# Expert weights of a job in four loads, each asked for when its half of the buffer is used up

## The reference

```python
def experts(x, gate_scores):                 # x: 16 samples x 256 tokens x 256 channels
    topk_w, topk_i = top_k(gate_scores, 2)   # two of four experts for each sample
    topk_w = topk_w / (topk_w.sum() + 1e-8)
    for e in range(4):
        h = gelu(x @ ew1[e] + eb1[e])        # 256 -> 1024
        y = h @ ew2[e] + eb2[e]              # 1024 -> 256
        out += w_be[:, e] * mask[e] * y
    return x + out + gelu(x @ sw1 + sb1) @ sw2 + sb2   # the shared expert, for all samples
```

## Time and profile before

| | us |
|---|---|
| median of three timed runs | 1384.66 (1384.63 to 1385.9) |
| the profiled execution's own time | 1386.06 |
| its span, first to last instruction | 1384.2 |
| expert jobs, first to last matmul start | 608.6 to 1008.1 |
| shared expert and recurrent network | from 1011.0 to the end |
| TensorE busy | 1227.4 (89% of the span) |
| VectorE busy | 883.5 (64%) |
| ScalarE busy | 633.3 (46%) |
| bytes read from HBM in the whole kernel | 160.66 MB |

### The profile page before, as it was taken

The page is one execution under the profiler, slowest core; times in us unless marked ns, Lnnn a source line. Parts: engine busy times, 40 slices in busy tenths (PEclk is TensorE's granted clock), DMA queues, the critical chain, the costliest instruction groups (busy, mean ns, idle before and its releaser), DMA issues.

```text
span 1384.2 us, 34408 instructions
## 1 busy us (share of the span) xinstructions
PE 1227.4 (89%) x14232; PEld 982.0 (71%) x14232; DVE 883.5 (64%) x2091; ACT 633.3 (46%) x1191; POOL 330.5 (24%) x311
## 2 busy tenths in 40 slices
PE   4489999999997878159899999999999999999996
PEld 2347676767664333049899999999988888888884
DVE  4978787878773499856565565656555555555552
ACT  2267777777775799413233333333323333333331
POOL 2554545454442399600000000000000000000000
PEclk9689999999999899659999999999999999999996
DMA  9212121212123000057888888888810000000000
GB/s 340 91 47 93 47 94 47 93 47 94 47 93 123 1 0 1 15 243 296 324 354 338 335 327 345 358 345 339 337 75 10 18 18 10 18 10 18 10 18 18
DMA packets 37898, 188.29 MB, mean 136 GB/s; under 512 B 3056, under 2 KB 13424, under 8 KB 29040
## 3 DMA queue, kind: packets, MB, share of 16 engines
q1 hardware_dynamic: 37744, 186.10, 35.1%
HBM read 160.66 MB, written 25.17 MB: 134 GB/s over the span
## 4 chain that ended last, share of the span: by engine, by line
PE 48%; DMA 4%; issue 3%; DVE 2%; ACT 0%; SPq 0%; POOLq 0%; POOL 0%; ACTq 0%
PE pr L1387 6%; PE py L1291 4%; DMA w<-weight_halves 4%; PE ph L1275 4%; PE ph L1276 4%; PE ph L1277 4%; PE py L1293 4%; PE py L1292 4%; PE pys L1426 4%; PE pys L1430 4%; PE phs L1413 2%; PE phs L1409 2%; PE phs L1411 2%; PE pys L1428 2%; PE pr L1398 2%
## 5 line engine op out<-in xcount | busy, mean ns | idle before, releaser
L1114 ACT ACTIVATE g<-ph,b 128x256 f32<-128x256 f32 x256 | 121.5, 475 | 273.5 <-PE ph L1277 273.5
L549 DVE TENSOR_REDUCE mx<-pR 128x4 f32<-128x1024 f32 x128 | 156.3, 1224 | 66.0 <-PE pR L707 64.5
L1222 DVE CAST ghi<-g 128x256 fp32r<-128x256 f32 x256 | 74.7, 292 | 154.0 <-ACT g L1114 153.8
L1493 DVE STREAM_TRANSPOSE preT<-pr 128x64 f32<-128x64 f32 x256 | 63.8, 249 | 163.4 <-PE pr L1387 163.0
L1291 PE MATMUL py<-ghi,w 128*128 128x256 f32 x512 | 147.6, 288 | 18.3 <-issue 16.9
L1275 PE MATMUL ph<-xhi,w 128*128 128x256 f32 x512 | 146.3, 286 | 17.3 <-DMA w<-weight_halves 17.3
L1468 ACT ACTIVATE hs<-preT 128x32 f32<-128x32 f32 x256 | 58.7, 229 | 199.6 <-DVE preT L1493 198.1
L1276 PE MATMUL ph<-xlo,w 128*128 128x256 f32 x512 | 145.9, 285 | 0.0
L1277 PE MATMUL ph<-xhi,w 128*128 128x256 f32 x512 | 145.8, 285 | 0.0
L1292 PE MATMUL py<-glo,w 128*128 128x256 f32 x512 | 145.3, 284 | 0.0
L1293 PE MATMUL py<-ghi,w 128*128 128x256 f32 x512 | 145.2, 284 | 0.0
(11 more groups left out here) (195 smaller groups left out, 2981.0 us busy)
## 6 DMA issues: line engine op xcount, KB each, us to landing
w<-weight_halves SPq DMA_DIRECT2D x66, 2048.0 KB, 12.0
weight_halves<-wparts SPq DMA_DIRECT2D x40, 512.0 KB, 4.1
modw<-in_ew SPq DMA_DIRECT2D x32, 256.0 KB, 4.6
xn<-in_x_tok SPq DMA_DIRECT2D x4, 1024.0 KB, 11.8
XT<-in_x_dm SPq DMA_DIRECT2D x2, 2048.0 KB, 14.2
out_dm<-staged SPq DMA_DIRECT2D x16, 256.0 KB, 2.0
modw<-in_sw SPq DMA_DIRECT2D x8, 256.0 KB, 4.3
modw<-in_mod_w SPq DMA_DIRECT2D x1, 768.0 KB, 7.1
```

The lines of the kernel that those rows point to most:

```text
L549: nc.vector.reduce_max(mx[:, :, 2 * j:2 * j + 2].rearrange("p t s -> p s t"), pR[k][:].rearrange("p s (t k) -> p s t k", t=TC), AX.X).then ...
L1114: nc.scalar.activation(g[:, t % RING], ph[t % RING][:, 0:T], ACT.Gelu_apprx_tanh, bias=b1[:, n, f:f + 1]).then_inc(gelu_done, 1)
```

## The change

`load_weights` makes four loads of 1 MB for each job where there were two of 2 MB. The inner width of 1024 is taken in two halves, h = 0 and h = 1 (four ticks each), and for each half the part of `w1` is loaded and then the part of `w2`. Each load has a wait of its own ahead of it: that of `w1` waits until the `up` ticks of that half of job n-2 are done, that of `w2` until its `down` ticks are. The waits in the caller are gone, also for job 32. A partition's half of `w1` is now four runs of 2 KB (high and low part by two halves of the channels), its half of `w2` two runs of 4 KB; before each was one run of 16 KB. The semaphores `w_in` get an index for the half, and TensorE waits at ticks 0 and 4 of a job, in `up` and in `down`, for the half that it goes into. `shared_and_rnn` waits for all four loads of job 32.

```diff
-        w_in = [[sem(st, f"w{w}_in{q}") for q in range(2)] for w in (1, 2)]
+        w_in = [[[sem(st, f"w{w}_in{h}{q}") for q in range(2)] for h in range(2)] for w in (1, 2)]
-        def load_weights(sp, n, src):
-
-            for w, dst, form in ((0, w1, "p v c f -> p (v c f)"), (1, w2, "p v c d -> p (v c d)")):
-                sp.dma_start(dst[:, n % 2].bitcast(fp32).rearrange(form), src[:, w].rearrange("o p v n -> p (o v n)"))\
-                    .then_inc(w_in[w][n % 2], 16)
+        def load_weights(sp, n, src, up, down):
+
+            for h in range(2):
+                lo, hi = h * FC // 2, (h + 1) * FC // 2
+                if n >= 2:
+                    sp.wait_ge(up, FC * (n - 2) + hi)
+                sp.dma_start(w1[:, n % 2, :, :, lo * P:hi * P].bitcast(fp32).rearrange("p v c f -> p (v c) f"),
+                             src[:, 0].rearrange("o p v (c f) -> p (o v c) f", c=DC)[:, :, lo * P:hi * P]).then_inc(w_in[0][h][n % 2], 16)
+                if n >= 2:
+                    sp.wait_ge(down, FC * (n - 2) + hi)
+                sp.dma_start(w2[:, n % 2, :, lo:hi].bitcast(fp32).rearrange("p v c d -> p v (c d)"),
+                             src[:, 1, :, :, lo * D:hi * D].rearrange("o p v n -> p (o v) n")).then_inc(w_in[1][h][n % 2], 16)
...
-                    if n >= 2:
-                        sp.wait_ge(down_done, FC * (n - 1))
-                    load_weights(sp, n, halves[bass.ds(e, 1)])
-                sp.wait_ge(down_done, FC * (JOBS - 1))
-                load_weights(sp, JOBS, halves[NE:NE + 1])
+                    load_weights(sp, n, halves[bass.ds(e, 1)], up_done, down_done)
+                load_weights(sp, JOBS, halves[NE:NE + 1], up_done, down_done)
...
-                        pe.wait_ge(w_in[0][n % 2], 16 * (n // 2 + 1))
+                    if f % (FC // 2) == 0:
+                        pe.wait_ge(w_in[0][2 * f // FC][n % 2], 16 * (n // 2 + 1))
...
-                    if f == 0:
-                        pe.wait_ge(w_in[1][n % 2], 16 * (n // 2 + 1))
-                        if n >= 2:
-                            pe.wait_ge(y_added, n - 1)
+                    if f % (FC // 2) == 0:
+                        pe.wait_ge(w_in[1][2 * f // FC][n % 2], 16 * (n // 2 + 1))
+                    if f == 0 and n >= 2:
+                        pe.wait_ge(y_added, n - 1)
...
-                pe.wait_ge(ex["w_in"][w][BUF], 16 * (TOP * B // 2 + 1))
+                for h in range(2):
+                    pe.wait_ge(ex["w_in"][w][h][BUF], 16 * (TOP * B // 2 + 1))
```

## The result

Four runs of the changed kernel beside four of the kernel before: 1354.67 us (1353.67 to 1359.35) against 1385.28 (1384.63 to 1387.12), 30.6 us less; the ratio is 0.9771, with an interval of 0.9746 to 0.9797. 1356 was forecast, in 1353.5 to 1372. The profiled execution took 1354.25 us, with a span of 1352.5.

A forecast was written before the change was run, and what follows sets the result against it. Late load requests, not DMA rate, were taken to hold back the DMA engines and so TensorE. Terms -25.2 - 2.2 - 1.2 = -28.6 us took the 1384.66 median to 1356.1; own range 1353.5 to 1359, overall 1353.5 to 1372.

The forecast's parts named there:

- (a): Expert weight loads: earlier requests give each half some 18 us from request to use, taking latency out of the sum.
- (b): Expert weight loads in shorter runs: the DMA engines need 10.5 to 10.9 us a job, under TensorE's 11.52.
- R: Time the DMA engines take to move one job's 4.19 MB of weights, taken as 10.5 to 10.9 us.
- the bound of 11.48: Value of R, 11.48 us or 365 GB/s, above which the DMA engines rather than TensorE set the pace.
- (c): Steady expert stage: with weights there, ticks run at 1.44 us throughout; term -25.2 us.
- (d): First expert job: the smaller first load lets the first `up` start earlier; term -2.2 us, from -1.1 to -2.8.
- The bad case: First job: the clock rises at the same absolute time as before, losing half of the 2.2 us again.
- (e): Hand-over to the shared expert: the load wait goes and the barrier is late next; term -1.2 us, not -2.6.
- (f): Added costs: two more TensorE waits a job and 132 SP loads for 66, 1.7 us of issuing in 11.5; term 0.
- The third one: Rival, slower: queue runs dry between loads, each dry spell costing 0.87 us; 14.0 us a job, 1439.5 us; chance 0.08.
- The second: Rival, no change: engines hold one load at a time and pay slow starts; 12.3 us a job, 1383.4 us; chance 0.05.
- The first rival: Rival: R over 11.52, DMA engines set the expert stage's pace; 1359 to 1381 us, 1372 at the bound; chance 0.13.

## Why the prediction was right

**(a) The cause.** That a late request, and not the rate, holds the engines back was right: with 340 GB/s turned into 365 the waits are gone. I had put it on the earlier request alone. The runs show that the halves alone do it too in the steady stage, since they move the need for the second half by four ticks; I had not reckoned that.

**(b) R.** 10.5 to 10.9 us were taken for a job. The rate with a full queue is 394 to 396 GB/s (640 to 680, and both runs with extra loads), 10.6 us. The prediction put the slowest engine 4% over the mean, by instruction fetches that all fall to one. An engine that falls behind is there, but by less: the landings with extra loads come at 12.1 and 13.5 us a job where the mean rate gives 11.9 and 13.3, 1 to 2%. The interpolation between the runs of 1 and of 3 KB held to 1%. With R at 10.6 to 10.9 the bound of 11.48 is 5 to 8% away: the run with 11.9 by the model lost 16 us in U to S.

**(c) The steady stage.** -25.2 was the term; U to S has 399.53 - 374.03 = 25.5.

**(d) The first job.** -2.2; P to U has 2.1, 2.2 and 2.1 in the three profiles. The landing was put at 5.7 us, and was 5.8. The bad case, that the clock would rise no sooner than before, didn't come: in the changed kernel it rose at 606, 4.1 us behind the first `up`, where the kernel before had it at 0.50 up to 617. Its first window, against rows 2:

```profile
600.00:617.00 17.00, 13.85 (x88) 12.56 (x89) 10.92 (x47) 4.97 (x9) 0.00 (x0) 0.82 1.02 370
```

It gained nothing, though. The 97th matmul starts 16.86 us behind the first in both kernels (618.75 - 601.89 and 625.47 - 608.61), so it isn't TensorE that paces the first job; that the earlier table load shortens it by 1.27 us points to the way through ScalarE and VectorE.

**(e) The hand-over.** -1.2 for the pause; it has 0.9. What I didn't see is the clock behind it, which costs up to 1.4 us in H to end (374.55 against 373.16) and nothing in the third profile; profiles without a fall differ by 0.9 us among themselves there (372.31 to 373.20).

**(f) What is added.** Right at 0, though SP needs 0.54 to 0.58 us for each of the short-run loads and not half of 0.85, so 2.2 us a job and not 1.7.

**The sum.** -28.6 stands against -27.0, -27.9 and -29.4 from P on. Between the medians it is 30.6 us, and 1354.67 lies 1.3 under the forecast: the scatter ahead of P, from 590 to 601 us, is larger than this miss, and the closeness to 1 us is luck in part. Timed twice more, the changed kernel had 1357.49 and 1359.27, and the kernel before 1386.6 and 1388.48 beside them: 29.1 and 29.2 us.

**What I said would show it.** Ticks and waits came as said. Slices of 390 to 410 GB/s follow one another only up to about 680; from then on dips to some 300 stand between them, since the engines are ahead and are paced by the requests, at 365. A DMA share near 1.0 I had named as the mark of a rate bound. It isn't: see below. **The rivals.** The third one's slow seams don't stay with a full queue, as argued: the runs with extra loads have 394 to 396 GB/s throughout. The second, 12.3 us a job, isn't borne out: loads of 1 MB that follow one another ran at 396 GB/s, and the eight of 0.5 MB at 366. The figure of the Trainium skill that the prediction set beside it, 341 GB/s for a load of 1 MB ("DMA: Bandwidth & Descriptors", section on measured bandwidth), is from loads issued by GpSimd, and its rule asks for 1 MB or more, which these loads meet; here they were issued by SyncE, and the measured 396 decides. The first rival's bound was crossed by the run with 0.5 MB more, 12.1 us a job: it lost 16 us in U to S.

## What to carry to other kernels

Where a double buffer is filled only once the whole buffer is free, look at the time from request to landing against the time from request to use: moving the request for one of the two loads by 3.6 us, without cutting a load, gave 25.4 of some 28 us. Cut a load only where somebody can begin with a part of it; a user that wants all parts at once, as the shared expert does, sees the last landing, and that is where the runs with late requests and with eight loads lost most of theirs. And cut a profile at fixed places before comparing spans: a stage that nobody touched moved by 10 us from run to run.

## What the runs showed of the hardware

- The DMA share of a stretch doesn't tell whether the engines are the limit. With loads of 1 MB it is 1.00 at 365 GB/s, where no one waits for them, and 1.04 at 394 to 396, where TensorE does; with 16 KB runs it is 0.92 at 365, and with eight loads a job 1.07 at 366. What tells is the rate against that of a full queue, and the waits.
- A load of 1 MB takes 5.8 us from an empty queue, 7.9 in the median of the changed kernel, and around 15.5 where the engines are the bound (15.7 for the last one with 0.5 MB more). The bytes account for 2.6 of it.
- A load lands with the last of sixteen engines, and with a full queue the engines drift apart: the sixteen counts of one load spread over 1.0 us at the start and over 6.4 at the end of the run with 0.5 MB more, at a mean rate that stays at 396 GB/s. With pauses between the requests, in the changed kernel, the last load's spread is 2.4 us.
- Behind a pause of TensorE of 2.0 us the granted clock fell to 0.5 for 3.4 us in two of three profiles of the changed kernel; behind one of 2.9 us in the kernel before it did not, and with those of 5.1 to 7.6 us it fell in all five profiles.
- SP takes 0.54 us to issue a load of 1 MB in runs of 2 or 4 KB and 0.34 for one of 2 MB in runs of 16 KB; with several loads waiting in the queue at the start, single issues took 2.8 and 3.5 us.
